# Self attention on one core: ACT instead of DVE copies the transposed values of units 1 to 7 into block form

## The reference

```python
x = x + cross_attention(layernorm(x), ctx[:, :64])   # 32 heads of 128, 8 key/value heads, rope, causal
x = x + self_attention(layernorm(x))                 # 32 heads of 16, causal, biases, output projection
x = x + moe_ffn(layernorm(x))                        # base layer, 8 thresholded low-rank experts
```

```python
q = (x @ Wq.T + bq).reshape(b, l, 32, 16).transpose(0, 2, 1, 3)     # k and v likewise
scores = jnp.einsum('bhqd,bhkd->bhqk', q, k) / math.sqrt(16)
att = jax.nn.softmax(jnp.where(causal, scores, -jnp.inf), axis=-1)
out = jnp.einsum('bhqk,bhkd->bhqd', att, v).transpose(0, 2, 1, 3).reshape(b, l, d)
return out @ Wo.T + bo
```

## Time and profile before

| | |
|---|---|
| runs of the kernel | 738.82, 738.43, 737.69 us; median 738.43 |
| the profiled execution | 738.54 us |
| its span in the profile | 736.7 us; the rest, 1.8 us, lies around the span |
| busy in the span | PE 710.8, PEld 565.4, DVE 520.8, ACT 371.9, POOL 485.9 us |
| granted TensorE clock | 0.998 of full speed |
| self attention's pairs | about 561 to 675 us |
| vc copies on DVE | 32 of 64x256, seven sets of four inside the loop over the pairs |

### The profile page before, as it was taken

One profiled execution on the slowest core, in us unless ns is written; L12 is line 12 of the kernel. 1 busy time (PEld: TensorE's weight loads), 2 busy tenths in 40 slices (PEclk: granted clock), 3 DMA queues, 4 the chain that ended last, 5 costly groups with the idle time before them and its releaser, 6 DMA issues.

```text
span 736.7 us, 12893 instructions
## 1 busy us (share of the span) xinstructions
PE 710.8 (96%) x4848; PEld 565.4 (77%) x4848; DVE 520.8 (71%) x815; ACT 371.9 (50%) x555; POOL 485.9 (66%) x366
## 2 busy tenths in 40 slices
PE   9999997799999999999999999989999999999897
PEld 7788886567787778787778778767787888877786
DVE  5756857766756757767757757757667887888855
ACT  5456645635544644743653554544246776653220
POOL 1898535678777776867867867746325799964440
PEclk9999999999999999999999999999999999999999
DMA  7553514031211310311301212200200110020003
GB/s 271 206 172 132 172 51 133 17 129 44 86 44 44 107 49 17 113 41 43 100 28 44 98 43 72 73 16 15 87 1 1 44 59 2 2 87 1 15 1 114
DMA packets 25561, 51.09 MB, mean 69 GB/s; under 512 B 2352, under 2 KB 10672, under 8 KB 25520
## 3 DMA queue, kind: packets, MB, share of 16 engines
q1 hardware_dynamic: 25520, 50.53, 20.8%
HBM read 40.04 MB, written 10.49 MB: 69 GB/s over the span
## 4 chain that ended last, share of the span: by engine, by line
PE 79%; DVE 7%; POOL 6%; ACT 3%; issue 3%; DMA 1%; SPq 0%; DVEq 0%; POOLq 0%
PE pj L1517 11%; PE sc L1610 9%; PE pj L1610 9%; PE pj L1708 8%; PE tp L1517 7%; PE pv L1503 6%; PE pv L1597 4%; PE tp L1610 4%; PE sc L1577 3%; PE tp L1491 2%; PE pj L1491 2%; PE sc L1758 2%; PE tp L1584 2%; PE tp L1771 2%; PE pv L1782 2%
## 5 line engine op out<-in xcount | busy, mean ns | idle before, releaser
L482 POOL TENSOR_TENSOR sw<-sw,cst 128x512 f32<-128x512 f32 x72 | 100.6, 1398 | 38.3 <-ACT sw L655 38.2
L1517 PE MATMUL pj<-x,w 128*128 128x512 f32 x384 | 103.5, 406 | 1.0 <-ACT pc L693 0.6
L506 POOL TENSOR_TENSOR sm<-sm,mx 128x512 f32<-128x512 f32 x64 | 72.0, 1131 | 45.5 <-DVE mx L1166 26.4
L1517 PEld LDWEIGHTS pj<-x,w 128*128 128x128 f32 x384 | 69.4, 189 | 24.6 <-DVE cq L1089 4.9
L500 POOL TENSOR_TENSOR w<-raw,w 128x896 fp32r<-128x896 f32 x28 | 60.9, 2196 | 34.6 <-ACT w L640 34.6
L511 POOL TENSOR_TENSOR sm<-sm,rz 128x512 f32<-128x512 f32 x64 | 65.9, 1043 | 19.5 <-DVE rz L1181 19.5
L1517 PE MATMUL tp<-x,w 128*128 128x512 f32 x288 | 76.2, 401 | 2.6 <-ACT sw L655 1.4
L488 POOL TENSOR_TENSOR qr<-t,sw 128x512 f32<-128x512 f32 x54 | 73.3, 1358 | 7.7
L775 ACT ACTIVATE sm<-sm 128x512 f32<-128x512 f32 x64 | 40.2, 631 | 69.2 <-POOL sm L506 69.2
L1708 PE MATMUL pj<-xh,ws 128*128 128x512 f32 x192 | 64.3, 401 | 0.2 <-ACT kb L863 0.2
L1517 PEld LDWEIGHTS tp<-x,w 128*128 128x128 f32 x288 | 51.9, 188 | 13.3 <-ACT sw L655 1.7
(11 more groups left out here) (268 smaller groups left out, 1799.3 us busy)
## 6 DMA issues: line engine op xcount, KB each, us to landing
rawd<-in_w_d SPq DMA_DIRECT2D x16, 512.0 KB, 3.3
raw<-in_w_q SPq DMA_DIRECT2D x15, 512.0 KB, 3.3
kscr<-sm SPq DMA_DIRECT2D x16, 256.0 KB, 2.2
vscr<-sm SPq DMA_DIRECT2D x16, 256.0 KB, 2.6
kr<-kscr SPq DMA_DIRECT2D x8, 512.0 KB, 3.3
vv<-vscr SPq DMA_DIRECT2D x16, 256.0 KB, 2.6
raw<-in_w_k SPq DMA_DIRECT2D x4, 512.0 KB, 6.2
cT<-in_ctxT SPq DMA_DIRECT2D x4, 512.0 KB, 7.4
```

The lines of the kernel that those rows point to most:

```text
L482: pool.tensor_tensor(bs(sw[par][:, :]), bs(sw[par][:, :]), rep(cst[:, C_SIN:C_SIN + S], HB), ALU.mult).then_inc(sin_done, 1)
L506: pool.tensor_tensor(s3, s3, per_group(mx[:, c, :], 8), ALU.subtract).then_inc(subbed, 1)
L1517: last = pe.matmul(bank, a, r, start=(start and k == 0 and part == 0), stop=(stop and k == 1 and part == 2), skip_group_check=True)
```

## The change

For v = 1 to 7 the four copies leave DVE's queue, where they stood behind the sums and reciprocals of the pair at c = 2, and enter ACT's queue, behind the pair's two exponentials and ahead of the key copies. The copies of unit 0 stay on DVE. The wait for the last memset moves with them.

```diff
@@ -880,6 +880,19 @@
                 act.wait_ge(pt_t, n + 1)
                 act.activation(pts[n % 2][:, :], tp[:, n % 2, :], ACT.Copy).then_inc(pt_done, 1)
 
+
+            def vc_copy(v):
+                if v == 1:
+                    act.wait_ge(zeroed, 4)
+                act.wait_ge(vt_t, v + 1)
+                src = tp[:, 0, :].rearrange("p (b t j d) -> p b t j d", b=4, t=2, j=2)
+                dst = vc[v % 2][:, :, :, :].rearrange("p (b o) t c -> p b o t c", o=2)
+                for j in range(2):
+                    for odd in range(2):
+                        last = act.activation(dst[64 * j:64 * j + 64, :, odd, :, 32 * j:32 * j + 32],
+                                              src[64 * odd:64 * odd + 64, :, :, j, :], ACT.Copy)
+                last.then_inc(vc_done, 1)
+
             def out_hi(v):
                 t, h = UNITS[v]
                 act.wait_ge(ssel, SCH * v + SCH)
@@ -932,6 +945,8 @@
                     if n + 2 < N_SS:
                         exp(N_SM + n + 2, (n + 2) % 4, S_SCALE)
                         exp(N_SM + n + 3, (n + 3) % 4, S_SCALE)
+                    if c == 2 and v + 1 < NSU:
+                        vc_copy(v + 1)
                 for i, at in LATE_AT.items():
                     if at == n + 1:
                         late_hi(i)
@@ -1379,10 +1394,6 @@
                         sum_rec(N_SM + n + 2, (n + 2) % 4)
                 if 2 * m in (OUT_AT + 2, OUT_AT + 4):
                     out_add_s((2 * m - OUT_AT - 2) // 2)
-                if c == 2 and v + 1 < NSU:
-                    if v == 0:
-                        dve.wait_ge(zeroed, 4)
-                    vc_copy(v + 1)
                 for n in pair:
                     if n + 4 < N_SS:
                         mask_max_s(n + 4)
```

## The result

The changed kernel took 742.76 us in the median of six runs (742.04 to 744.86), the kernel before beside it 738.44 us. The ratio is 1.0065, with a 95% interval of 1.0048 to 1.0081: slower by 0.65%, 4.8 us by the ratio and 4.3 by the medians. A later group of runs gave 741.94 us against 739.73, ratio 1.0024 (1.0015 to 1.0033). The profiled execution took 742.11 us.

The account below looks back on a forecast made before the run. PE was taken as the bound until ACT's copies made a loop slower than its 14.88 us: exp(26) 3.6 us later, less 0.67 in the tail, +3.0 on the 738.43 us median, 741.4 us; range 737.8 to 745.5 us.

Parts of the forecast that it names:

- What bounds the kernel: Self attention: PE alone is the chain from 568.57 to 648.14 us, POOL has no slack, the stage's tail is latency bound.
- DVE's relief: DVE, units 1 to 6: time freed from four copies of 1.68 us each unit becomes idle time, worth nothing.
- The tail gain of 0.67 us: Unit 7: the mask addition of n = 30 starts at about 662.37 us instead of 663.04, gaining 0.67 us.
- The price of the copies, 1.62 us: ACT at c = 2: four 64x256 copies, 0.40 us each without overlap, take 1.62 us with the gap.
- The loop: exp(n0+2) to exp(n0+6) through DVE, POOL and ACT: laps of 15.3 to 16.4 us exceed PE's 14.88; exp(26) 3.6 us late.
- PE's waits: PE waits for kb before values projections at about 605.5, 636 and 652 us, some 1 us each.
- The sum: Whole kernel: 3.6 us later at exp(26), less 0.67 in the tail, gives +3.0 us, 741.4 us.
- the overlap on ACT: Rival: ACT's four copies overlap and take 1.26 us; result +0.8, 739.2 us; chance 0.18.
- the loop doesn't close: Rival: scores and mask additions pace POOL, each unit starts afresh, kb's slack hides the copies; 737.8 us; chance 0.09.
- kb's price: Rival: short runs of 32 elements make ACT's four copies cost 2.74 us like kb's; +9.7, 748.1 us; chance 0.09.
- the whole 1.68 us in the tail: Rival: DVE's freed 1.68 us counts whole in the tail if n = 30's scores come sooner; 736.7 us; chance 0.05.
- The loads of late weights: SP's loads start up to some 3 us later; without a unit's lead, the late high part holds ACT up to 3 us once.

Follow-up runs that it names:

- the fourth experiment: Changed kernel with POOL's late low parts and the bias addition of n = 12 moved behind the next n's subtractions: 738.76 us, ratio 0.9990.
- act_load: Kernel before plus four additional 64x256 copies on ACT for each of units 1 to 6, DVE keeping the real ones: 743.50 us, ratio 1.0055.
- unit7_only: Kernel before with only unit 7's copies moved to ACT, DVE keeping units 0 to 6: 738.55 us, ratio 0.9988.
- twice: Changed kernel with ACT's four copies made twice, first into scratch space, then into vc: 752.87 us, ratio 1.0192.
- odd_units: Kernel before with ACT making the copies for units 1, 3, 5 and 7, DVE those for 0, 2, 4 and 6: 741.03 us, ratio 1.0010.
- after_again: Changed kernel run once more, unaltered, beside the kernel before: 741.94 us, ratio 1.0024.

## Why the prediction was right, point by point

- **What bounds the kernel**: right. PE was the bound up to 648 us, and POOL the second engine without slack; the fourth experiment shows that POOL's work between normalise and subtract decides.
- **DVE's relief is worth nothing in units 1 to 6**: shown by act_load, where DVE kept the copies and the loss was the same.
- **The tail gain of 0.67 us**: 0.54 measured (10.16 to 9.62 us), and 0.58 in unit7_only. I had let the mask start 0.06 us behind the end of the scores counted less their modelled overlap; it starts 0.07 behind the full end (665.46 + 1.10 = 666.56, mask 666.63). The other 0.05 us is the scores, which start 8.45 us behind exp(26) here and 8.40 before.
- **The price of the copies, 1.62 us**: 1.55. One takes 378 ns (380 forecast), and the starts are 0.39 us apart: on 64 partitions with changing start partitions they don't overlap, as the swap pairs had said. By the Trainium skill ("ScalarE: Activation LUTs", What ACT_TABLE_LOAD costs), back-to-back ACTIVATEs overlap by about 93 ns, which gave an estimate of 1.3 us and a result of about 739.5 us, +1.1, where the trace has +3.04. The trace agrees with it for 128 partitions (0.60 us long, 0.49 apart) and not for these copies.
- **The loop**: laps forecast 15.3, 15.3, 15.3, 16.4, 15.8 us; measured 15.25, 15.28, 15.45, 16.37, 15.80. Its start moved by 1.57 us (9.14 from exp(4) to exp(6) against 7.57) for 1.62. Exp(26) is 3.58 us late for 3.6. That it fits so closely is partly luck: the copies were 0.07 us cheaper in each lap, and the other terms 0.2 us longer in all, most of it at v = 3 (from the second exponential to the copies 0.64 us for 0.54). Six times the price was confirmed by twice (9.61 us for 6 x 1.56).
- **PE's waits**: forecast about 605.5, 636 and 652 us, some 1 us each; they are at 607.1, 637.9 and 654.2 us with 0.90, 0.73 and 0.90 us. The times are later by the 0.55 us of start-up and clock and by the waits themselves. POOL waited more for rz, as forecast: 16.8 us between 560 and 680 us, against 10.8.
- **The sum**: +3.0 us forecast (741.4), +3.04 in the trace, +3.2 to 3.6 at equal mean clock. The medians of the first runs say +4.3 (742.76), inside the range of 737.8 to 745.5. The term that is missing is the clock: the time depends on how many stretches at 1.2 GHz there are and where they fall, and the prediction has nothing for it. That it explains the rest of the 4.3 us is inferred: of the kernel before, only the profiled run of that group has its clock on record.
- **Rivals**: the overlap on ACT fell by the rows, "the loop doesn't close" by the laps, kb's price by the 378 ns, the whole 1.68 us in the tail by the 0.54. The loads of late weights, which could have held ACT up to 3 us more, didn't: no lap holds such a wait.
- What I had wrong only showed in an experiment: the slack of laps without copies. I had let a lap shrink to its own sum. In odd_units exp(18) came at its place of before, but its sum on DVE had to wait for the selections (623.32 us, 1.12 behind the exponential), and the normalisation for POOL's bias addition as well (624.38); and the next lap can't end ahead of DVE's own copies for unit 6.

## What to carry to other kernels

An engine that is half idle can still stand on a path that closes on itself: add up the path from one of its instructions to the same one a round later, and compare with the bound's round. In this kernel moved work was free below that, and above it each us counted once per round; a single lap above it was made up by shorter ones, where some were left before the tail (units 1 and 3). Before work is moved to it, see what else lies in the lap: here reordering POOL, not unloading ACT, made room. And work taken from an engine behind a wait is worth only what that wait leaves.

## What the runs showed of the hardware that I had not expected

- Granted clock: stretches at 1.2 GHz appear in otherwise identical code at different places. The thirteen traces have them at 121 to 129 us, at about 496 us, or both, and six again between 659 and 699 us; PE came out of idle times of 0.3 to 2.7 us just ahead of them, or was still idle. What one costs depends on what comes behind it. At 124 us it was nothing, as PE waits there anyway; at 496 us 0.95 to 1.02 us of PE's lag, in all nine traces that have it; near 687 and 698 us 1.1 us; in the tail 1.6 us (exp(26) to exp(30) took 13.75 us in after_again and 12.19 us in the change's first profile). The ratio of the same two kernels was 1.0065 in one group of runs, where 2 of 6 runs of the changed kernel had the higher mean clock, and 1.0024 in another, where 6 of 11 had it.
- Copies on 64 partitions: from PSUM 378 ns, 0.39 us apart; from SBUF 415 ns, 0.42 us apart. Neither overlaps with its neighbour, on an engine whose copies on 128 partitions follow each other 0.1 us before the end. If it is the number of partitions or the change of the start partition that does this, no run here separates.
